# Attention outputs transposed by DMA as 16-bit planes, instead of by TensorE

## Chip, cores and metric

The kernel runs on one core of a Trainium2 chip. The metric is device time in microseconds (us) of one execution; lower is better. TensorE (PE, with PEld for its weight loads), VectorE (DVE), ScalarE (ACT), GpSimd (POOL) and SyncE (SP, which here only issues transfers) each run their own list of instructions in order and wait for each other through semaphores.

## Reference

Two batches of 2048 tokens, width 512, are a gated cross-attention block followed by a quantised feed-forward block:

```python
scores = einsum('bhid,bhjd->bhij', LN(x) @ Wq, ctx @ Wk) * scale      # 16 heads of 32, 77 context rows
x1  = x + tanh(g0) * (softmax(scores) @ (ctx @ Wv)) @ Wo
xq  = fake_quant_int8(LN(x1), one scale from max|LN(x1)| over everything)
h   = fake_quant_int8(silu(xq @ Wgate_q.T) * (xq @ Wup_q.T), one scale from max|h|)
out = x1 + tanh(g1) * (h @ Wdown_q.T)          # weights quantised to int8, one scale a row
```

The maximum over all of |LN(x1)| has to be known before the first quantised product.

## The kernel before

Three stages follow each other in blocks: attention, gate/up, down. The change lies in the attention block. It handles 32 tiles of 128 tokens in a hand-written software pipeline of slots; each engine has its own function `slot(n, t)`, called for n = 0 to 35 by `tile_slots` (L345): slots 0 to 3 and 20 on are written out, slots 4 to 19 are a hardware loop of 4 rounds of 4 slots, in which semaphore values are computed from the loop register.

In slot n TensorE does, in this order: the first half of the scores of tile n; the transpose of the outputs of tile n-2 (`out_transpose`, L1028: four 128x128 transposes from `o_sb` into PSUM `p_x`); two of the three groups of transposes of the probabilities of tile n-1 (`prob_transpose`, L994); half of the queries of tile n+2; the outputs of tile n-1 for the first 8 heads; the second half of the scores of tile n; the last group of transposes; the other half of the queries; the outputs of the other 8 heads; and the projection by Wo of tile n-2 (`project`). Products that need float32 precision are three products of high and low parts (`three`).

VectorE works through the same slot: `scores_max` and `scores_sub` (subtracts the row maximum and writes `prob[t % 2][:, half, :]`; L701) for half 0, the addition of the projection to x1, `bn_stats` of x1, the low part of the transposed outputs (`out_part`, L722 on), the row maximum of a gate/up weight row block `w_in`, the normalised outputs of tile n-1 (`outputs_rec`, `outputs_norm`, L714), then the same for half 1, the maximum of |LN(x1)| (`xmax`), the low part of the queries, the statistics of tile n+6 and the low part of the transposed tokens (`x_part`). In slots 22 to 29 there are instead parts of the quantisation of the down weights (`down_part`), in even slots the maxima (k = 0), in odd slots the int8 values (k = 1).

ScalarE writes high parts, copies the transposed probabilities (`pT`), takes the exponentials, and writes |LN(x1)| of tile n-4 into PSUM `p_y` (`xabs`, L188).

From tile 8 on the normalised tokens are transposed by DMA: GpSimd splits the float32 tile `xn` into two planes of 16 bits in `xpl_u` (`x_split`, L458), SP transposes the planes back into `xn` in 16-bit units (`planes_transposed`, L371), and ScalarE joins the planes again to float32 (`x_join`, L556). SP's queue holds these transposes in one order with the loads of weight rows (`rows`), their transposes (`rows_transposed`), and in slots 21 to 29 the loads (`down_rows`, three transfers) and stores (`down_stored`) of the down weights.

GpSimd also computes the deviations (`deviation`, `deviation2`) and casts the int8 weights to bfloat16 (L506, L515); before the second cast of a down row block it waits for the store of the first, since both use `w_bf`.

Of the kernel before, what the change touches and what calls it, by code (L numbers as in the profile page):

```python
# [5 lines left out]
F32 = mybir.dt.float32  # L6
# [10 lines left out]
P = 128  # L17
B = 2
S = 2048
D = 512  # L20
# [47 lines left out]
PLANES_FREE = NT - 4  # L68
# [3 lines left out]
def flamingo_block(nc, x, ctx_in, mask, g_xattn, g_ffn, Wq, Wk, Wv, Wo, clip_x, clip_down,  # L72
# [8 lines left out]
    with top:  # L81
# [11 lines left out]
        sb, _, sem = tensors(top)  # L93
        x1 = sb("x1", [P, NT, D])
# [16 lines left out]
        with attn:  # L111
# [17 lines left out]
            with work:  # L129
# [5 lines left out]
                prob = [sb(f"prob{i}", [P, 2, HW]) for i in range(2)]  # L135
                pT = sb("pT", [P, 2 * KB, P])
                o_sb = sb("o_sb", [P, D])
# [45 lines left out]
                xpl_planes = xpl_u[:, :].rearrange("p (two n) -> p two n", two=2)  # L183
# [3 lines left out]
                def xabs(m):  # L187


                    return xpl[:, :] if isinstance(m, int) and m >= PLANES_FREE - 4 else p_y[:, :]  # L190

# [37 lines left out]
                t_warm = sem("t_warm")  # L229
# [81 lines left out]
                a_xpl = sem("a_xpl")  # L311
                g_wbf = sem("g_wbf")
# [11 lines left out]
                def wait(eng, sem_, value):  # L324

                    if not isinstance(value, int) or value > 0:
                        eng.wait_ge(sem_, value)  # L327

# [33 lines left out]
                def _(sp):  # L362
# [8 lines left out]
                    def planes_transposed(n):  # L371
                        sp.wait_ge(g_xpl, n - DIRECT + 1)
                        sp.dma_start_transpose(xn_u[:, :].rearrange("p (c n) -> p c n", n=P),
                                               xpl_u[:, :]).then_inc(d_xT, 16)
# [48 lines left out]
                    planes_transposed(NW + 3)  # L423
# [18 lines left out]
                    planes_transposed(NW + 4)  # L442
                    for r in range(KD):
                        if WD0 + 2 * r + 5 < NT:
                            planes_transposed(WD0 + 2 * r + 5)
# [4 lines left out]
                        if WD0 + 2 * r + 6 < NT:  # L450
                            planes_transposed(WD0 + 2 * r + 6)
                        down_stored(r, WC - 1)
                    sp.wait_ge(d_wT, 16 * NW)
# [3 lines left out]
                def _(pool):  # L457
                    def x_split():  # L458
                        pool.tensor_copy(xpl_planes, xn_pairs).then_inc(g_xpl, 1)

                    def deviation(n, t, split=False):
# [4 lines left out]
                        if split:  # L466
                            wait(pool, a_xn, n)
                            wait(pool, v_xlo, n - 1)
                        else:
                            wait(pool, a_xn, n - 1)  # L470
                        pool.tensor_tensor(ve[:, :], mv[:, 1:2], eps[:, :], ALU.add).then_inc(g_self, 1)
                        pool.tensor_tensor(nmean[:, :], mv[:, 0:1], minus[:, :], ALU.mult).then_inc(g_self, 1)
                        if split:
                            x_split()
# [5 lines left out]
                    def deviation2(m):  # L480
# [7 lines left out]
                        wait(pool, g_self2, 3 * m + 3)  # L488
                        pool.tensor_tensor(nb2[:, span(m)], nmean2[:, :], rs2[:, span(m)], ALU.mult)\
                            .then_inc(g_nb2, 1)  # L490

                    def slot(n, t):
                        if runs(n + 5, NT):
                            deviation(n + 5, t + 5, split=joined(n + 4))
                        elif runs(n + 4, NT):
                            wait(pool, a_xn, n + 5)
                            wait(pool, v_xlo, n + 4)
                            x_split()
                        if runs(n - 3, NT):
                            deviation2(n - 3)  # L500
# [40 lines left out]
                def _(act):  # L541
# [13 lines left out]

                    def x_join(n, t):  # L556
                        wait(act, d_xT, (n - DIRECT) * 16 + 16)
                        act.copy(xpl_pairs, xn_planes).then_inc(a_xpl, 1)
# [9 lines left out]
                    def slot(n, t):  # L568
                        if runs(n - 2, NT):
                            wait(act, t_oT, n - 1)  # L570
                            if not last_tile(n - 2):
# [1047 lines left out]
```

## Time and profile before

| | |
|---|---|
| median of 3 runs | 642.82 us (642.26 to 643.49) |
| the profiled execution, its own time | 643.5 us |
| its span | 641.7 us |
| PE busy | 623.3 us (97%) |
| DVE busy | 510.4 us (80%) |
| ACT busy | 352.6 us (55%) |
| POOL busy | 197.2 us (31%) |
| attention block, slots 4 to 19 | 71.36 to 249.03 us |
| attention block, slots 22 to 29 | 271.26 to 360.17 us |

Busy shares are averages over three stages with different limits, and a busy PE is one that has instructions in flight. A row of busy time by stretch has: the stretch, its length, busy us and instructions (x) of PE, PEld, DVE, ACT and POOL, the granted clock of TensorE (1.00 is 2.4 GHz), the mean busy share of the DMA engines, GB/s. In a timeline the second column is the duration of one instruction; neighbours on an engine overlap a little, so the difference of two starts says what an instruction takes of its engine's time.

### The profile page before, as it was taken

Reading aid. Unit: us, or ns where it says so; the run is one execution under the profiler, and the core shown is the slowest. Engines: PE = TensorE matmul, PEld = TensorE weight load, DVE = VectorE, ACT = ScalarE, POOL = GpSimd, SP = SyncE. Lnnn points to the kernel's source line nnn. Section 1 sums busy time; section 2 is a strip of 40 time slices with the busy share of each in tenths; the row PEclk is TensorE's granted clock in tenths of the full one; section 3 lists DMA queues with packets and bytes.
Section 4 is the critical chain, followed back from the end, with each engine's and each line's share of the span. In section 5 each row is a group of like instructions: output and inputs, shape, how many; then the busy total and the mean of one; then the engine's idle time right before and its main releaser. Section 6 shows DMA issues by size and latency. Waiting matters only on the chain. (4 is left out here: it accounts for less than half of the span.)

```text
span 641.7 us, 12724 instructions
## 1 busy us (share of the span) xinstructions
PE 623.3 (97%) x3912; PEld 471.1 (73%) x3912; DVE 510.4 (80%) x954; ACT 352.6 (55%) x512; POOL 197.2 (31%) x416
## 2 busy tenths in 40 slices
PE   8969999999999999999999997999999999899997
PEld 6769999999999999999999995444444444444544
DVE  6586889888888989899887766788888888866764
ACT  5254465667666565666664343555555554365653
POOL 7021333333333333232320211201111110056775
PEclk9999999999999999999999998999999999999999
DMA  8739222222222223313411000276446110099723
GB/s 311 193 80 335 59 52 59 65 57 65 58 65 50 63 51 59 90 39 85 95 33 60 25 0 1 49 226 211 135 145 212 25 32 9 1 344 394 275 105 126
DMA packets 85206, 69.61 MB, mean 108 GB/s; under 512 B 64915, under 2 KB 67373, under 8 KB 85165
## 3 DMA queue, kind: packets, MB, share of 16 engines
q1 hardware_dynamic: 80259, 52.33, 29.1%
q10 hardware_dynamic: 4906, 16.78, 7.4%
q8 instruction: 21, 0.34, 0.2%
q14 instruction: 20, 0.16, 0.1%
HBM read 32.48 MB, written 21.36 MB: 84 GB/s over the span
## 5 line engine op out<-in xcount | busy, mean ns | idle before, releaser
L1298 ACT ACTIVATE sb_silu<-ps_g,sb_sgu 128x512 f32<-128x512 f32 x88 | 60.5, 687 | 72.1 <-PE ps_g L1385 43.8
L1385 PE MATMUL ps_g<-sb_xqT,sb_wgu 128*128 128x512 bf16 x352 | 90.3, 379 | 0.6 <-DVE sb_xqT L1341 0.6
L1385 PE MATMUL ps_u<-sb_xqT,sb_wgu 128*128 128x512 bf16 x352 | 90.3, 379 | 0.0
L589 ACT COPY sb_pT<-ps_p 128x512 f32<-128x512 f32 (+1 forms) x96 | 46.5, 520 | 71.3 <-PE ps_p L1002 71.3
L1356 DVE SCALAR_TENSOR_TENSOR sb_h<-ps_u,sb_sgu,sb_silu 128x512 f32<-128x512 f32 (+1 forms) x88 | 66.0, 751 | 19.4 <-PE ps_u L1385 18.3
L1013 PE MATMUL ps_o<-sb_vblk,sb_pT 128*128 (+4 forms) x640 | 79.0, 270 | 1.2 <-ACT sb_pT L589 1.2
L1013 PEld LDWEIGHTS ps_o<-sb_vblk,sb_pT 128*128 128x128 f32 (+1 forms) x640 | 76.8, 191 | 1.8 <-ACT sb_pT L589 1.4
L946 PE MATMUL ps_q<-sb_xT_hi,sb_wq_hi 128*128 128x256 f32 x256 | 77.5, 303 | 0.0
L698 DVE TENSOR_REDUCE sb_smax<-ps_s 128x8 f32<-128x616 f32 x64 | 51.1, 799 | 26.8 <-PE ps_s L991 26.4
L948 PE MATMUL ps_q<-sb_xT_hi,sb_wq_lo 128*128 128x256 f32 x256 | 72.3, 282 | 0.0
L947 PE MATMUL ps_q<-sb_xT_lo,sb_wq_hi 128*128 128x256 f32 x256 | 72.2, 282 | 0.0
L1591 PE MATMUL ps_z<-sb_wdT,sb_hq 128*128 128x512 bf16 x330 | 71.7, 380 | 0.0
L1466 POOL TENSOR_TENSOR sb_wgu<-sb_wgu,sb_x 128x512 f32<-128x512 f32 x31 | 53.7, 1734 | 53.5 <-DVE sb_wgu L1523 53.0
L1360 DVE TENSOR_REDUCE sb_hmax<-sb_h 128x1 f32<-128x512 f32 (+1 forms) x88 | 60.4, 686 | 8.0 <-DVE sb_h L1356 0.7
L1385 PEld LDWEIGHTS ps_g<-sb_xqT,sb_wgu 128*128 128x128 bf16 x352 | 34.4, 98 | 42.1 <-ACT sb_xqT L1312 0.8
L1385 PEld LDWEIGHTS ps_u<-sb_xqT,sb_wgu 128*128 128x128 bf16 x352 | 34.4, 98 | 41.5
L1591 PEld LDWEIGHTS ps_z<-sb_wdT,sb_hq 128*128 128x128 bf16 x330 | 32.4, 98 | 39.1 <-issue 0.8
L1486 ACT CAST sb_hq<-sb_h 128x1408 bf16<-128x1408 int8 (+1 forms) x32 | 42.0, 1311 | 28.9 <-DVE sb_h L1516 28.3
L593 ACT ACTIVATE sb_prob<-sb_prob 128x616 f32<-128x616 f32 x64 | 46.2, 721 | 16.1 <-DVE sb_prob L704 16.1
L704 DVE TENSOR_TENSOR sb_prob<-ps_s,sb_smax 128x616 f32<-128x616 f32 x64 | 50.8, 793 | 2.7
L1281 POOL CAST sb_xqb<-sb_xq 128x512 bf16<-128x512 int8 x28 | 17.2, 613 | 111.8 <-ACT sb_xq L1290 95.4
L946 PE MATMUL ps_y<-sb_wo_hi,sb_oT_hi 128*128 128x512 f32 x124 | 51.4, 414 | 0.0
(218 smaller groups left out, 1349.8 us busy)
## 6 DMA issues: line engine op xcount, KB each, us to landing
h_spill<-sb_h SPq DMA_DIRECT2D x4, 2816.0 KB, 8.8
sb_h<-h_spill ACTq DMA_DIRECT2D x16, 704.0 KB, 6.7
out_dram<-sb_wgu SPq DMA_DIRECT2D x31, 256.0 KB, 2.2
sb_x<-in_x_dram ACTq DMA_DIRECT2D x1, 4096.0 KB, 17.0
sb_w_in<-in_L_ffn_w_gate_dram SPq DMA_DIRECT2D x11, 256.0 KB, 2.6
sb_w_in<-in_L_ffn_w_up_dram SPq DMA_DIRECT2D x11, 256.0 KB, 2.6
sb_x<-in_x_dram SPq DMA_DIRECT2D x2, 1024.0 KB, 14.1
sb_x<-in_x_dram SPq DMA_DIRECT2D x2, 512.0 KB, 4.7
```

The lines of the kernel that those rows point to most:

```text
L698: dve.tensor_reduce(smax[:, half, :].rearrange("p (g h) -> p g h", g=2), half_scores(), X, ALU.max).then_inc(v_max, 1)
L704: dve.tensor_tensor(prob[t % 2][:, half, :].rearrange("p (g h m) -> p g h m", g=2, h=HG), half_scores(), smax[:, half, :].rearrange("p (g ...
L946: pe.matmul(o, hi, rhi, start=first, stop=False)
L947: pe.matmul(o, hi, rlo, start=False, stop=False)
L948: return pe.matmul(o, lo, rhi, start=False, stop=last)
L1013: last = pe.matmul(p_o[:, first:end + 1, :].rearrange("p h d -> p (h d)"), pT[rows, half * KB + j, :], vblk[rows, span(b), half, SLOT0[j]: ...
L1298: act.activation(silu[(j * KI + i) % 2][:, :, :].rearrange("p t n -> p (t n)"), p_g[(j * KI + i) % 2][:, :], ACT.Silu, scale=sgu[:, i:i + ...
L1356: dve.scalar_tensor_tensor(steps_h, p_u[(j * KI + i) % 2][:, :, :], sgu[:, KI + i:KI + i + 1], silu[(j * KI + i) % 2][:, :, :], ALU.mult, ...
L1360: dve.tensor_reduce(hmax[:, span(u)], steps_h, mybir.AxisListType.XY, ALU.max, apply_absolute_value=True).then_inc(v_hmax, 1)
L1385: last = pe.matmul(banks[(j * KI + i) % 2][:, :], wgu[:, what, k, i * P:(i + 1) * P], xqT[j][:, k, :], start=(k == 0), stop=(k == KD - 1))
L1466: pool.tensor_tensor(yd[k], yd[k], x1[:, span((v + RT) % NT), :].rearrange("p a d -> p (a d)"), ALU.add).then_inc(g_out, 1)
L1591: last = pe.matmul(p_z[k % 4][:, :], hq[k % 4][:, i, :], wdT[:, i, :], start=(i == 0), stop=(i == KI - 1))
```

## The change

Tiles 2 to 29 (`O_FIRST`, `O_END`) are no longer transposed by TensorE. Their outputs lie in `o_sb`, seen as 16-bit words. GpSimd splits each half (8 heads) into planes (`out_split`), which lie in half 0 of the probabilities' buffer of the same parity; SP transposes each half by a DMA of its own (`out_transposed`) back into `o_sb`; ScalarE joins both halves into `xpl` (`out_join`) and makes the high part from it. The token tile's planes now lie in half 1 of the probabilities' buffer, and |LN(x1)| too, instead of PSUM `p_y` or `xpl`. Some work is put in another order: on ScalarE the first exponential and |LN(x1)|, on VectorE the weight row's maximum, `out_part`, `xmax`. Unused semaphores go.

```diff
@@ SP
+                    def out_transposed(m, half):
+                        sp.wait_ge(g_opl, 2 * (m - O_FIRST) + half + 1)
+                        sp.dma_start_transpose(o_pairs(half).rearrange("p (c n) -> p c n", n=P),
+                                               o_planes(m, half)).then_inc(d_oT, 16)
+
+                    def slot_transposes(n):
+                        if o_joined(n - 2):
+                            out_transposed(n - 2, 1)
+                        if DIRECT <= n + 4 < NT:
+                            planes_transposed(n + 4)
+                        if o_joined(n - 1):
+                            out_transposed(n - 1, 0)
@@ order on SP: weights up to slot 22, then the down weights
                         rows_transposed(w - 2)
-                        if w + 3 >= DIRECT:
-                            planes_transposed(w + 3)
+                        slot_transposes(w - 1)
                         rows(w)
...
                     down_rows(0)
-                    planes_transposed(NW + 4)
+                    slot_transposes(NW)
                     for r in range(KD):
-                        if WD0 + 2 * r + 5 < NT:
-                            planes_transposed(WD0 + 2 * r + 5)
+                        slot_transposes(WD0 + 2 * r + 1)
                         for q in range(WC - 1):
                             down_stored(r, q)
                         if r + 1 < KD:
                             down_rows(r + 1)
-                        if WD0 + 2 * r + 6 < NT:
-                            planes_transposed(WD0 + 2 * r + 6)
+                        slot_transposes(WD0 + 2 * r + 2)
                         down_stored(r, WC - 1)
@@ GpSimd
+                    def out_split(t, half):
+                        pool.tensor_copy(o_planes(t, half).rearrange("p (two n) -> p two n", two=2),
+                                         o_pairs(half).rearrange("p (n two) -> p two n", two=2)).then_inc(g_opl, 1)
...
+                        wait(pool, a_xn, n - 1)
+                        if o_ready:
+                            wait(pool, v_o, 2 * (n - 6))
+                        pool.tensor_tensor(ve[:, :], mv[:, 1:2], eps[:, :], ALU.add).then_inc(g_self, 1)
+                        if o_ready:
+                            out_split(t - 7, 1)
+                        if x_ready:
                             wait(pool, a_xn, n)
+                            wait(pool, t_p, 3 * (n - 6))
+                            wait(pool, v_xmax, n - 8)
...
                         pool.tensor_tensor(nb2[:, span(m)], nmean2[:, :], rs2[:, span(m)], ALU.mult)\
                             .then_inc(g_nb2, 1)
+                        if o_joined(m + 2):
+                            out_split(t + 2, 0)
@@ ScalarE
+                    def out_join(m):
+                        wait(act, d_oT, 32 * (m - O_FIRST + 1))
+                        wait(act, v_xlo, min(m + 6, NT) if isinstance(m, int) else m + 6)
+                        act.copy(xpl_halves, o_halves).then_inc(a_opl, 1)
+                        wait(act, a_opl, m - O_FIRST + 1)
+                        wait(act, t_y, m)
+                        act.copy(oT(m)[0], xpl_T).then_inc(a_ohi, 1)
@@ VectorE, scores_sub
+                        if half == 0 and o_joined(n - 2):
+                            wait(dve, d_oT, 32 * (n - 1 - O_FIRST))
+                        if half == 1:
+                            wait(dve, v_xmax, n - 3)
+                        if half == 1 and runs(n + 4, NT) and joined(n + 4):
+                            wait(dve, d_xT, 16 * (n + 5 - DIRECT))
@@ VectorE, outputs_norm
-                        wait(dve, t_oT, n)
+                        if o_joined(n - 1):
+                            wait(dve, a_opl, n - O_FIRST)
@@ VectorE, slot: the weight row's maximum now stands ahead of scores_sub(n, t, 0), out_part behind
@@ outputs_norm(n - 1, 0), the reduction for xmax behind scores_sub(n, t, 1)
@@ TensorE
-                        if not isinstance(m, int) or m < PLANES_FREE - 2:
-                            wait(pe, v_xmax, m)
...
-                        if runs(n - 2, NT - 1):
+                        if runs(n - 2, NT - 1) and not o_joined(n - 2):
                             out_transpose(n - 2)
```

## Rows read from the trace of the kernel before

**Rows 1.** Busy time by engine in slots 4 to 19 and 22 to 29.

```profile
71.36:249.03 177.67, 177.67 (x1313) 169.27 (x1312) 152.69 (x320) 113.87 (x176) 63.98 (x174) 1.00 0.26 60
...
271.26:360.17 88.91, 88.91 (x658) 84.64 (x657) 78.14 (x163) 51.72 (x82) 25.56 (x69) 1.00 0.25 65
```

**Rows 2.** Timeline of PE, slot 19: start us, duration us, instruction.

```profile
238.77 0.60 PE L1036 MATMUL ps_x<-sb_identf,sb_o_sb 128*128 128x128 f32 x4
239.21 1.04 PE L1002 MATMUL ps_p<-sb_identf,sb_prob 128*128 128x128 f32 x8
...
242.54 0.39 PE L989 MATMUL ps_s<-sb_k_hi,sb_q_hi 128*128 x1
```

**Rows 3.** Timeline of DVE, slot 19.

```profile
240.50 0.80 DVE L704 TENSOR_TENSOR sb_prob<-ps_s,sb_smax 128x616 f32<-128x616 f32 x1
...
242.40 0.67 DVE L818 TENSOR_REDUCE sb_w_am<-sb_w_in 128x1 f32<-128x512 f32 x1
243.00 0.17 DVE L822 BATCH_NORM_AGGREGATE sb_mvt<-sb_bn 128x2 f32<-128x6 f32 x1
...
247.49 0.42 DVE L717 TENSOR_TENSOR sb_o_sb<-ps_o,sb_rden 128x256 f32<-128x256 f32 x1
247.83 0.17 DVE L663 BATCH_NORM_AGGREGATE sb_mv<-sb_bn 128x2 f32<-128x6 f32 x1
248.87 0.69 DVE L676 TENSOR_TENSOR sb_xT_lo<-sb_xpl,sb_xT_hi 128x512 fp32r<-128x512 f32 x1 [0.87 <-ACT sb_xT_hi L561]
```

**Rows 4.** Timeline of POOL behind that instruction.

```profile
249.79 0.19 POOL L471 TENSOR_TENSOR sb_ve<-sb_mv,sb_eps 128x1 f32<-128x1 f32 x1 [3.87 <-DVE sb_xT_lo L676]
```

**Rows 5.** POOL's 16-bit split and a cast of 512 columns, by shape.

```profile
L459 POOL COPY sb_xpl<-sb_xn 128x1024 uint16<-128x1024 uint16 x24 | 24.9, 1036 | 5.1 <-DVE sb_xT_lo L676 5.1
...
L515 POOL CAST sb_w_bf<-sb_vblk 128x512 bf16<-128x512 int8 x4 | 2.5, 614 | 7.8 <-DMA wd_spill<-sb_w_bf 7.8
```

**Rows 6.** DMA transposes of the page: count, median us from issue to landing.

```profile
sb_xn<-sb_xpl SPq DMA_TRANSPOSE x24, 3.1
...
sb_wgu<-sb_w_bf SPq DMA_TRANSPOSE x22, 2.6
```

**Rows 7.** ACT's join of the token planes.

```profile
L558 ACT COPY sb_xpl<-sb_xn 128x1024 uint16<-128x1024 uint16 x24 | 32.3, 1346 | 0.0
```

**Rows 8.** Timeline of DVE, slots 23, 24 and 26: first subtraction, second normalisation.

```profile
284.85 0.80 DVE L704 TENSOR_TENSOR sb_prob<-ps_s,sb_smax 128x616 f32<-128x616 f32 x1
...
288.14 0.80 DVE L698 TENSOR_REDUCE sb_smax<-ps_s 128x8 f32<-128x616 f32 x1 [0.25 <-PE ps_s L991]
...
292.40 0.42 DVE L717 TENSOR_TENSOR sb_o_sb<-ps_o,sb_rden 128x256 f32<-128x256 f32 x1
...
295.96 0.80 DVE L704 TENSOR_TENSOR sb_prob<-ps_s,sb_smax 128x616 f32<-128x616 f32 x1
...
304.15 0.42 DVE L717 TENSOR_TENSOR sb_o_sb<-ps_o,sb_rden 128x256 f32<-128x256 f32 x1
...
318.19 0.80 DVE L704 TENSOR_TENSOR sb_prob<-ps_s,sb_smax 128x616 f32<-128x616 f32 x1
...
325.81 0.42 DVE L717 TENSOR_TENSOR sb_o_sb<-ps_o,sb_rden 128x256 f32<-128x256 f32 x1
```

**Rows 9.** Timeline of SP's queue, end of slot 23 and start of slot 24.

```profile
292.06 0.43 SPq L431 DMA_DIRECT2D sb_w_in<-in_L_ffn_w_down_dram  x1
...
293.02 0.43 SPq L431 DMA_DIRECT2D sb_w_in<-in_L_ffn_w_down_dram  x1
295.70 1.23 SPq L373 DMA_TRANSPOSE sb_xn<-sb_xpl  x1
```

**Rows 10.** Stretch in which these loads move (columns as in Rows 1).

```profile
292.40:295.80 3.40, 3.40 (x26) 3.17 (x25) 2.47 (x5) 2.54 (x5) 1.43 (x4) 1.00 0.79 248
```

**Rows 11.** DVE's int8 instructions of 512 columns, by shape, 80 to 340 us.

```profile
L742 DVE TENSOR_SCALAR sb_vblk<-sb_vblk,sb_wd_inv 128x512 int8<-128x512 f32 x3 | 1.8, 607 | 0.0
...
L742 DVE TENSOR_SCALAR sb_w_i<-sb_w_in,sb_wd_inv 128x512 int8<-128x512 f32 x3 | 1.4, 477 | 0.0
```

More of the change, by code:

```diff
@@ L134, in flamingo_block @@
                 xn = xn_u[:, :].bitcast(F32)
-                prob = [sb(f"prob{i}", [P, 2, HW]) for i in range(2)]
+                prob_u = [sb(f"prob{i}", [P, 2, 2 * HW], U16) for i in range(2)]
+                prob = [a[:, :, :].bitcast(F32) for a in prob_u]
                 pT = sb("pT", [P, 2 * KB, P])
-                o_sb = sb("o_sb", [P, D])
+                o_u = sb("o_sb", [P, 2 * D], U16)
+                o_sb = o_u[:, :].bitcast(F32)
                 oT_hi = sb("oT_hi", [P, KD, P], F32R)
@@ L576, in slot @@
                         for c, (k0, k1) in enumerate(CHUNKS):
-                            if c == 2 and runs(n - 4, NT - 1):
-                                wait(act, g_nb2, n - 3)
-                                wait(act, v_xmax, n - 3)
-                                if isinstance(n, int) and n >= PLANES_FREE:
-                                    act.wait_ge(v_xlo, NT)
-                                else:
-                                    wait(act, v_x1, n - 2)
-                                act.activation(xabs(n - 4), row(n - 4), ACT.Abs, bias=nb2[:, span(n - 4)],
-                                               scale=rs2[:, span(n - 4)]).then_inc(a_abs, 1)
+                            if c == 2 and runs(n - 2, NT) and o_joined(n - 2):
+                                out_join(n - 2)
+                            if c == 2 and runs(n, NT):
+                                exponential(n, t, 0)
                             if runs(n - 1, NT):
@@ L589, in slot @@
                                 act.copy(pT[:, k0:k1, :], p_p[c % 2][:, 0:k1 - k0, :]).then_inc(a_p, 1)
-                        for half in range(2):
-                            if runs(n, NT):
-                                wait(act, v_sub, 2 * n + half + 1)
-                                act.activation(prob[t % 2][:, half, :], prob[t % 2][:, half, :], ACT.Exp,
-                                               scale=SCALE).then_inc(a_exp, 1)
-                            if half == 0 and runs(n + 2, NT):
-                                q_part(n + 2, (t + 2) % 4)
+                        if runs(n - 4, NT - 1):
+                            wait(act, g_nb2, n - 3)
+                            wait(act, v_xmax, n - 3)
+                            wait(act, t_p, 3 * min(n, NT) if isinstance(n, int) else 3 * n)
+                            act.activation(xabs(t), row(n - 4), ACT.Abs, bias=nb2[:, span(n - 4)],
+                                           scale=rs2[:, span(n - 4)]).then_inc(a_abs, 1)
+                        if runs(n + 2, NT):
+                            q_part(n + 2, (t + 2) % 4)
+                        if runs(n, NT):
+                            exponential(n, t, 1)
                         if runs(n + 4, NT):
@@ L830, in slot @@
                             outputs_norm(n - 1, 0)
+                        if runs(n - 2, NT - 1) and o_joined(n - 2):
+                            out_part(n - 2)
                         if runs(n, NT):
@@ L1063, in slot @@
                             scores(n, t, 0)
-                        if runs(n - 2, NT - 1):
+                        if runs(n - 2, NT - 1) and not o_joined(n - 2):
                             out_transpose(n - 2)
```

113 lines of the change are left out of this document (69 added, 44 removed).

## The prediction

> **What bounds the kernel now.** I first read the busy time of each engine by stretch, cut at the starts of slots. In slots 4 to 19 TensorE is busy for all 177.67 us, in slots 22 to 29 for all 88.91 us [rows 1], with a granted clock of 1.00 (2.4 GHz): a slot is 177.67 / 16 = 11.10 us there and 88.91 / 8 = 11.11 us here. So TensorE sets the pace of the attention block, and only what leaves its list shortens it. VectorE is close behind: 152.69 / 16 = 9.5 us a slot in the first stretch, 78.14 / 8 = 9.8 us in the second. Next the timelines of single slots, for the distances between VectorE's instructions, because the new waits tie these into a circle; last the transfers, with their time from issue to landing.
>
> **What goes.** The four transposes of the outputs start 0.44 us before the next group (238.77, 239.21) [rows 2]. TensorE has no gap around them, so a slot of TensorE would take 11.10 - 0.44 = 10.66 us. It happens in slots 4 to 31, 28 times: 12.3 us at most.
>
> **What comes, and the circle.** `scores_sub(n, t, 0)` now waits until both halves of tile n-2 have been transposed, since their planes lie in the buffer that it writes. The second half of tile n-2 is normalised at the end of slot n-1. Call S the start of the first subtraction and N the start of the second normalisation in a slot. Then S, VectorE's list up to N, split, transpose, and the next S follow each other, and the period of a slot is the longer of TensorE's 10.66 us and this circle.
>
> S to N is 247.49 - 240.50 = 6.99 us in slot 19 [rows 3]. The weight row's maximum is moved ahead of S: 243.00 - 242.40 = 0.60 us less, so 6.39 us.
>
> N to the next S, written-out slots: normalisation and aggregate 247.83 + 0.17 - 247.49 = 0.51 [rows 3]; the hand-over to POOL 249.79 - (248.87 + 0.69) = 0.23 [rows 3, 4], say 0.2; POOL's first small instruction 0.15 (0.19 long [rows 4]); the half's split between half of the whole one, 0.52, and a cast of 512 columns, 0.61: 0.6, as an instruction has a fixed part [rows 5]; the transpose 2.6, as the weights' have the same 128x512 elements (the token's, twice as large, take 3.1 [rows 6]; 2.6 is the nearest); SP's start and VectorE's release about 0.1 (estimate). Together 4.2 us, bounds 3.6 (less at both hand-overs and 0.2 us less in flight) and 4.8 (a transpose as slow as the large one). In the loop three more waits with computed values stand behind the one that ends last; I add 0.15, between 0 and 0.35 (estimate).
>
> The half's split on POOL also meets VectorE's int8 instruction. Where such an instruction met a cast on POOL it took 607 ns, otherwise 477 [rows 11]; I add 0.13, between 0 and 0.4.
>
> Slots 4 to 19: 6.39 + 0.13 + 4.35 = 10.87 us, just above TensorE's 10.66. Gain 11.10 - 10.87 = 0.23, x 16 = 3.7 us (bounds 0 and 7.0). Slot 20 gains 0.4, slots 30 and 31, where VectorE has much less to do, 0.44 each: together 5.0 us.
>
> **Slots 21 to 29.** Here VectorE has the down weights' work between S and N. Even slots: 304.15 - 295.96 = 8.19 in slot 24 [rows 8], + 4.2 = 12.39, which is 1.28 us over 11.11; slots 22 and 24: +2.6. Slots 26 and 28 have no token statistics: 325.81 - 318.19 = 7.62 [rows 8], and the split waits for no aggregate: 3.95; 11.57, +0.46 each: +0.9.
>
> Odd slots: 292.40 - 284.85 = 7.55, less the 0.25 us in which VectorE waited for scores [rows 8]. But SP's queue comes later than this. The three loads of the next down rows start 292.06 - 284.85 = 7.21 us behind S [rows 8, 9]. In front of the first store now stand a split (0.6) and the issue of a transpose (1.23 [rows 9], 0.6 of it beyond the cast), while `out_part` is gone from VectorE's list there (-0.5): the loads start at S + 7.9 and occupy SP's queue to S + 9.35 (293.02 + 0.43 - 292.06 = 1.4 [rows 9]). Only then can the second half be issued. Landing, if its data meet nothing: 9.4 + 2.6 + 0.1 = S + 12.1. If they stand behind the loads, whose data moved from 292.4 to 295.8 [rows 10], so to S + 11.65: + (2.6 - 1.23) + 0.1 = 13.1. I take 13.0, as all sit in one queue: +1.9 us for slots 23, 25 and 27, +5.7. Slot 29 has no loads behind it: -0.3. Slot 21 has the loads for row block 0 in the same place: +1.0 (bounds -0.4 and +1.5). Together 2.6 + 0.9 + 5.7 - 0.3 + 1.0 = 9.9 us.
>
> The Trainium skill ("DMA: Bandwidth & Descriptors", Two DMAs through the same engine are not ordered) says that descriptors of one queue of a DMA engine start in order. By that the half stands behind the loads, 13.1; no row here has a transpose right behind loads.
>
> **What costs nothing, and its cover.** ACT gets a second join of 1.35 us [rows 7]: 51.72 / 8 + 1.35 = 7.8 us of a slot of over 10.6 [rows 1]. `out_join` ends about 2.1 us behind the landing; VectorE comes to `out_part` 2.0 us behind S, and TensorE's projection is more than 2 us later. POOL's two splits, 1.2 us, are added to 64 / 16 = 4 us. On TensorE the subtraction has 242.54 - 241.30 = 1.24 us before the second scores [rows 2, 3]; 0.44 and 0.60 of that go, and 0.2 is left: a late landing reaches TensorE almost at once. The token's planes are issued behind the half, 1.2 us later than the earliest; their reader on VectorE comes some 4 us after S. |LN(x1)| from SBUF instead of PSUM, the renamed semaphores and the moved exponential: 0.
>
> **Sum.** 9.9 - 5.0 = +4.9 us on the profiled execution, 643.5 to 648.4. The median of the runs is 0.7 us below it, so 647.5 us. What a measurement here can tell from no change is about 0.2%, 1.3 us.
>
> **Rivals.**
> 1. Faster: the half's way is short. At N to S of 3.6 us slots 4 to 19 are bound by TensorE (16 x 0.44 = 7.0, with slots 20, 30 and 31 8.3); slots 22 and 24 cost 1.4, 26 and 28 -0.3, the odd ones 3.9 (the loads' data less in the way), 21 and 29 nothing: 5.0. Net -3.3: 639.5 us. It decides below about 3.95 us. For it: two of the terms are bounds from other shapes. Against it: 2.6 us of it is measured 22 times [rows 6].
> 2. The new waits don't reach TensorE anywhere: 28 x 0.44, 630.5 us. Against it: 8.19 us from S to N leaves 2.5 us for a 2.6 us transpose.
> 3. The circle is longer, since VectorE and POOL get into each other's way. VectorE's `x_part` (0.69 us, both inputs in SBUF) starts 248.87 - 247.49 = 1.4 us behind N [rows 3], after the change about 0.8, because the second exponential comes earlier; the split would start at N + 1.0. If the split waits for it to end, 0.45 us are added in 16 slots and 0.33 in slots 22, 24 and 26: +8.2, 655.7 us. Neither for nor against it is there a row with such a pair; the 607 ns above speak for some cost. The Trainium skill ("SBUF — State Buffer", Who interferes with whom) has it as a rule that a VectorE instruction with two SBUF inputs contends with a GpSimd instruction that reads SBUF, and that the second one blocks; by it this rival is what happens.
> 4. Both halves nearly cancel: slots 4 to 19 reach TensorE's pace, the down slots cost what I say: -8.3 + 9.9, or a little less; 641.5 to 644.1.
>
> **Chances.** Forecast (644.1 to 651) 0.45; longer circle (above 651) 0.18; short way (637 to 641.5) 0.20; near cancelling 0.12; nothing reaches TensorE 0.05. Faster 0.25, same 0.12, slower 0.63. The range must take in most of the longer circle, to 656, and most of the short way, from 639; what is left out is the last case and the outer ends. The forecast's own range is 644 to 651.
>
> **What would show it.** TensorE idle in front of the second scores (L989), released by the subtraction; VectorE idle in front of the first subtraction, released by the transpose into `o_sb`; slot lengths of 10.7 to 11.0 us in slots 4 to 19, some 12.4 and 13.0 in turn in slots 22 to 25; PE busy in the second stretch well under its length. The half's split at 0.6 us, its landing at 2.6. The prediction is wrong if N to S is below 4 us, or if the down slots take 11 us.

## The result, and the profile after the change

The changed kernel takes 658.9 us (median of 4 runs, 657.6 to 661.9) against 642.7 us (642.3 to 643.5) for the kernel before: a ratio of 1.0258, 95% interval 1.0231 to 1.0286. It is slower by 16.2 us, where 4.8 us were forecast and the range ended at 656. The profiled execution is the longest of the four, 661.85 us with a span of 659.7 us; before, the span was 641.7 us.

S is the start of the first subtraction of a slot and N that of the second normalisation, as in the prediction. From S of slot 4 to S of slot 31 the trace before shows 372.68 - 73.94 = 298.74 us, the one after 389.33 - 72.44 = 316.89 us: 18.15 us more, as much as the spans differ by (18.0 us). Ahead of slot 4 the trace after is 1.5 us shorter and behind S of slot 31 1.35 us longer (269.02 and 270.37 us), which nearly cancels, so the loss lies between slots 4 and 31. Busy time by engine of the changed kernel, slots 4 to 19, 20 and 21, 22 to 30 (columns as in [rows 1]):

```profile
72.44:251.58 179.14, 175.02 (x1251) 164.71 (x1250) 153.81 (x321) 136.51 (x193) 94.25 (x208) 0.99 0.40 82
251.58:275.34 23.76, 22.78 (x169) 21.57 (x168) 19.89 (x40) 17.17 (x25) 11.02 (x26) 1.00 0.46 103
275.34:380.03 104.69, 93.80 (x620) 88.87 (x620) 78.52 (x163) 62.25 (x90) 38.34 (x80) 0.90 0.30 69
```

In [rows 1] TensorE was busy for the whole of both stretches. Now it is idle for 4.1 us of the first stretch, 1.0 us of the second and 10.9 us of the last, and its granted clock in the last is 0.90. The waits of the changed kernel (total us, times, longest us) name the instruction:

```profile
DVE sb_prob L775 <- DMA sb_o_sb<-sb_prob: 27.5, 22, 4.2
PE ps_s L1066 <- DVE sb_prob L775: 18.1, 12, 3.4
```

VectorE's subtraction waits for the transpose into `o_sb`, and TensorE's second scores for the subtraction. Slot 10 shows the circle at rest. Timelines of DVE, of POOL and of SP's queue:

```profile
142.14 0.80 DVE L775 TENSOR_TENSOR sb_prob<-ps_s,sb_smax 128x616 f32<-128x616 f32 x1 [0.44 <-DMA sb_o_sb<-sb_prob]
...
148.57 0.42 DVE L791 TENSOR_TENSOR sb_o_sb<-ps_o,sb_rden 128x256 f32<-128x256 f32 x1
148.91 0.17 DVE L728 BATCH_NORM_AGGREGATE sb_mv<-sb_bn 128x2 f32<-128x6 f32 x1
149.36 0.69 DVE L741 TENSOR_TENSOR sb_xT_lo<-sb_xpl,sb_xT_hi 128x512 fp32r<-128x512 f32 x1 [0.28 <-ACT sb_xT_hi L630]
...
153.05 0.80 DVE L775 TENSOR_TENSOR sb_prob<-ps_s,sb_smax 128x616 f32<-128x616 f32 x1 [0.44 <-DMA sb_o_sb<-sb_prob]
```

```profile
149.25 0.19 POOL L504 TENSOR_TENSOR sb_ve<-sb_mv,sb_eps 128x1 f32<-128x1 f32 x1 [2.00 <-DVE sb_mv L728]
149.38 1.15 POOL L493 COPY sb_prob<-sb_o_sb 128x512 uint16<-128x512 uint16 x1
```

```profile
150.55 1.19 SPq L397 DMA_TRANSPOSE sb_o_sb<-sb_prob  x1
```

S to N is 6.43 us (predicted 6.39). N to S is 4.48 us: 0.68 to POOL's start, 0.13 for its small instruction, 1.15 for the split, 2.5 from issue to landing. The split takes nearly twice the 0.6 us of the sum, and it starts while VectorE's `x_part` with two inputs in SBUF runs. The period is 10.91 us. Slots 9, 13, 14, 17 and 18 look the same. In slots 8, 11, 12, 15 and 16 POOL's small instruction is the one beside `x_part`: it takes 0.67 us in slot 8 and 0.69 us in slot 11, and the split 0.60 and 0.61. In slot 19 POOL begins first, and VectorE's instruction is the long one:

```profile
248.34 0.61 POOL L493 COPY sb_prob<-sb_o_sb 128x512 uint16<-128x512 uint16 x1
...
248.40 1.10 DVE L741 TENSOR_TENSOR sb_xT_lo<-sb_xpl,sb_xT_hi 128x512 fp32r<-128x512 f32 x1 [0.28 <-ACT sb_xT_hi L630]
```

Slot 23 is one of the three that cost most. SP's queue, POOL and DVE:

```profile
292.09 1.19 SPq L397 DMA_TRANSPOSE sb_o_sb<-sb_prob  x1
293.33 3.05 SPq L468 DMA_DIRECT2D wd_spill<-sb_w_bf  x2
296.42 0.43 SPq L462 DMA_DIRECT2D sb_w_in<-in_L_ffn_w_down_dram  x1
...
297.39 0.43 SPq L462 DMA_DIRECT2D sb_w_in<-in_L_ffn_w_down_dram  x1
297.87 1.19 SPq L397 DMA_TRANSPOSE sb_o_sb<-sb_prob  x1
```

```profile
291.46 0.61 POOL L493 COPY sb_prob<-sb_o_sb 128x512 uint16<-128x512 uint16 x1
292.01 0.81 POOL L564 CAST sb_w_bf<-sb_w_i 128x512 bf16<-128x512 int8 x1
295.40 0.61 POOL L564 CAST sb_w_bf<-sb_vblk 128x512 bf16<-128x512 int8 x1 [2.58 <-DMA wd_spill<-sb_w_bf]
...
296.55 0.61 POOL L493 COPY sb_prob<-sb_o_sb 128x512 uint16<-128x512 uint16 x1
```

```profile
287.75 0.80 DVE L775 TENSOR_TENSOR sb_prob<-ps_s,sb_smax 128x616 f32<-128x616 f32 x1 [1.00 <-DMA sb_o_sb<-sb_prob]
...
301.92 0.80 DVE L775 TENSOR_TENSOR sb_prob<-ps_s,sb_smax 128x616 f32<-128x616 f32 x1 [4.06 <-DMA sb_o_sb<-sb_prob]
```

In front of the second half stand the issue of the first half, the first store, POOL's second cast (which waits 2.58 us for that store to land), the second store and the three loads. The half is issued 297.87 - 287.75 = 10.12 us behind S, and the next S starts 4.05 us after the issue.

### The profile page after: what moved, and what is told of

It is laid out like the page before. It is cut to its first block and busy times, and to the rows that moved or that the text cites. A ratio compares the mean times of both kernels' runs of the same rounds, so it can differ in the third digit from the quotient of the medians.

```text
span 659.7 us, 12770 instructions
## 1 busy us (share of the span) xinstructions
PE 622.3 (94%) x3779; PEld 467.5 (71%) x3800; DVE 512.6 (78%) x954; ACT 391.6 (59%) x540; POOL 247.8 (38%) x472
## 5 line engine op out<-in xcount | busy, mean ns | idle before, releaser
L1023 PE MATMUL ps_q<-sb_xT_hi,sb_wq_hi 128*128 128x256 f32 x256 | 80.2, 313 | 0.0
L1025 PE MATMUL ps_q<-sb_xT_hi,sb_wq_lo 128*128 128x256 f32 x256 | 74.6, 291 | 0.0
L1024 PE MATMUL ps_q<-sb_xT_lo,sb_wq_hi 128*128 128x256 f32 x256 | 74.6, 291 | 0.0
L1066 PE MATMUL ps_s<-sb_k_hi,sb_q_hi 128*128 128x308 f32 (+1 forms) x128 | 43.5, 339 | 20.4 <-DVE sb_prob L775 18.1
L619 ACT COPY sb_xpl<-sb_o_sb 128x1024 uint16<-128x1024 uint16 x28 | 37.7, 1348 | 34.0 <-DMA sb_o_sb<-sb_prob 34.0
```

The lines of the kernel that those rows point to most:

```text
L1023: pe.matmul(o, hi, rhi, start=first, stop=False)
L1024: pe.matmul(o, hi, rlo, start=False, stop=False)
L1025: return pe.matmul(o, lo, rhi, start=False, stop=last)
```

## The experiments

All times are medians; each ratio is against the kernel before on the same chip (642.2 to 642.5 us). The changed kernel's 658.9 us were measured beside 642.7 us for the kernel before, so up to 0.5 us of a difference between a version and the changed kernel can come from that. The expectations name the experiments by labels: 1 is e1_end19, 2 e2_rest_alone, 3 e3_split_first, 4 e5_xpart_waits, 5 e4_half_before_loads, 9 e9_split_end19, 10 e10_best and 12 e12_both_queues. Slot lengths are those from S to S in each run's own trace.

**1. Fewer joined tiles.**

```diff
-O_FIRST, O_END = 2, NT - 2
+O_FIRST, O_END = 2, 19
```

> The changed kernel with its list of joined tiles cut to 2 to 18 (O_END = 19 instead of 30); tiles 19 to 31 are transposed by TensorE again, everything else stays. Theory (the loss arises in the slots with down weights, through the wait of the first subtraction on the outputs' halves): slots 4 to 19 take 10.9 to 11.2 us as in the changed kernel (11.10 before), slots 20 to 30 take 11.1 us again: about 2 us under the kernel before, 640.5 us; 644 if the long slots 5 to 7 (11.9 to 12.6 us) of the profiled run return. Rival (the loss comes from the other parts, the token's planes and |LN(x1)| in the probabilities' buffer, or the moved exponential): slots 21 to 29 stay long, 655 us or more.

Measured 642.4 us (ratio 0.9998, 0.9978 to 1.0018). Slots 21 to 29 are back at 11.1 us (slot 21 at 10.63). Slots 4 to 19 take 179.00 us, as in the changed kernel, with the long slots 5 to 7 (11.71, 12.55, 11.92). So the down slots carry 16.5 us, the whole difference between this kernel and the changed one, and the loop's slots, predicted to gain 3.7 us, lose 1.4. The theory of the slots held. The other parts were tested by themselves:

**2. Everything but the outputs.** `o_joined` is false for every tile.

> No outputs are joined at all (all tiles' outputs are transposed by TensorE); what is left of the change is the token's planes and |LN(x1)| in the probabilities' buffer, the weight row's maximum ahead of the first subtraction and the exponential in front of the third chunk. Theory: these cost nothing, 642.7 us within 1.3. Rival: they carry a part of the 16 us; then this kernel shows that part.

Measured 641.95 us, ratio 0.9999 (0.9989 to 1.0008): the token's planes and |LN(x1)| in the probabilities' buffer and the moved exponential, weight row's maximum and `xmax` cost nothing. `out_part` has its new place only for joined tiles, so this run doesn't test that.

**3. The split ahead of the statistics.**

```diff
+    if o_ready:
+        wait(pool, v_o, 2 * (n - 6))
+        pool.tensor_tensor(dum[:, :], eps[:, :], minus[:, :], ALU.mult)
+        out_split(t - 7, 1)
     wait(pool, v_st, n + 1)
...
-    if o_ready:
-        out_split(t - 7, 1)
```

> In slots 4 to 26 POOL splits the second half as soon as it is normalised, ahead of its wait for the token's statistics and of the first small instruction (one small instruction carries the wait). Theory (the circle sets the slots, and the split is long because it runs beside VectorE's x_part with both inputs in SBUF: 1.15 us instead of 0.60): split 0.60 us, second normalisation to first subtraction 3.8 us instead of 4.45; slots 4 to 19 fall from 10.9 to TensorE's 10.66, slots 21, 22 and 24 by 0.7 each, the odd down slots hardly: about 6 us less than the changed kernel, 652.5 us. First rival (the meeting only moves to another instruction of VectorE): 0.35 us less in the circle, 655 us. Second rival (TensorE or the clock sets slots 4 to 19): within 1 us of 658.9.

Measured 655.2 us, ratio 1.0208 (1.0188 to 1.0229). Slots 8 to 19 fall from 131.57 to 128.43 us, 10.70 each, and slots 4 to 7 from 47.57 to 44.98. Slots 21 and 22 stay at 12.89 and 12.39, where 0.7 less was expected, slot 24 grows from 12.40 to 13.31 (its clock is 0.74, see experiment 7), and the odd down slots stay at 13.6 to 15.5. The total lies at the first rival's, but the trace tells the two apart: in slots 9 to 11, 13 to 15 and 17 to 19 the split takes 0.61 us and it is VectorE's `x_part` that is stretched, to 0.99 to 1.01 us, without making S late. The meeting has moved, as the rival says, but out of the circle, as the theory says; only in slots 4, 8, 12 and 16 is the split still 1.13 to 1.14 us. What is missing from the total is missing in the down slots.

**4. `x_part` behind the split.** The order on POOL is unchanged; only the meeting is taken away.

```diff
     if runs(n + 4, NT):
+        if o_joined(n - 1):
+            wait(dve, g_opl, 2 * (n - O_FIRST))
         x_part(n + 4, t)
```

> The changed kernel, but VectorE's x_part in slots 4 to 27 starts only when POOL has split the second half of the outputs, so the two never run at once; POOL's order is that of the changed kernel. Theory (the split takes 1.15 instead of 0.60 us because of an instruction of VectorE with both inputs in SBUF beside it, and the circle sets the slots): split 0.60 us, second normalisation to first subtraction about 4.0 us instead of 4.45, slots 4 to 19 10.66 instead of 10.9, slots 22 and 24 0.45 less: 5 us less than the changed kernel, 654 us. Rival (the split is long for another reason, or x_part is so late that the queries wait for it): the split stays above 1 us or the time within 1 us of 658.9.

Measured 651.2 us, ratio 1.0127 (1.0107 to 1.0148), 7.7 us under the changed kernel, where 5 were expected. DVE and POOL in slot 11 of this kernel:

```profile
156.11 0.42 DVE L791 TENSOR_TENSOR sb_o_sb<-ps_o,sb_rden 128x256 f32<-128x256 f32 x1
...
157.72 0.69 DVE L741 TENSOR_TENSOR sb_xT_lo<-sb_xpl,sb_xT_hi 128x512 fp32r<-128x512 f32 x1 [1.10 <-POOL sb_prob L493]
...
160.23 0.79 DVE L775 TENSOR_TENSOR sb_prob<-ps_s,sb_smax 128x616 f32<-128x616 f32 x1
```

```profile
157.07 0.61 POOL L493 COPY sb_prob<-sb_o_sb 128x512 uint16<-128x512 uint16 x1
157.84 0.62 POOL L511 TENSOR_TENSOR sb_nmean<-sb_mv,sb_minus 128x1 f32<-128x1 f32 x1 [0.15 <-issue]
```

The split is back at 0.61 us although `x_part` is as long as before (0.69); the stretching has moved to a small instruction that nobody waits for (0.62 instead of 0.19), and S waits no more. N to S is 4.12 us. Slots 8 to 19 take 127.84 us, 10.65 each, TensorE's pace; slots 4 to 7 fall from 47.57 to 43.91 us. Of the long slots only slot 6, 11.62 us, is left. The edit takes the meeting away from the split and, to do so, starts `x_part` some 0.7 us later. In slots 8 to 19 the gain of 3.73 us fits the meeting. About as much, 3.66 us, lies in slots 4 to 7, and these are not steady: with the same wait they take 44.21 us in experiment 12 and 46.29 us in experiment 13. So that part of the 7.7 us isn't shown to be the meeting's alone. Slots 22 and 24 were to fall by 0.45 us each; slot 22 falls to 12.18, slot 24 grows to 13.65 us. In it TensorE is busy at a clock of 0.75 (window with TensorE alone):

```profile
295.37:309.02 13.65, 12.70 (x71) 0.75 0.23 41
```

**5. The second half in front of the loads.**

```diff
+    if o_joined(WD0 + 2 * r):
+        out_transposed(WD0 + 2 * r, 1)
     if r + 1 < KD:
         down_rows(r + 1)
-    slot_transposes(WD0 + 2 * r + 2)
+    slot_transposes(WD0 + 2 * r + 2, first=False)
```

and the same around `down_rows(0)`.

> In the queue that issues all of these transfers the second half of the outputs is issued in front of the three loads of the next down rows (in slots 20, 21, 23, 25, 27 and 29), not behind them. Theory (the odd down slots are long because the half waits behind the loads and is issued 10.1 us after the first subtraction): slots 23, 25 and 27 fall from 14.2 to 14.9 us to about 12.4, slot 21 by 0.4; TensorE's idle times of 3.3 us shrink to about 1.7 and the granted clock stays at 1.00, so slots 26 and 28 fall from 12.3 to 11.6: 8 us less, 651 us. Rival (the loads come too late for the next row block's first maximum): as much is given back in the even slots, 657 to 659 us.

Measured 659.0 us, ratio 1.0277 (1.0248 to 1.0307). Slots 21, 23, 25 and 27 fall to 10.81, 12.02, 12.01 and 11.46 us, and the even ones rise to 14.45, 14.23, 13.72 and 14.12: the rival. DVE in slot 22:

```profile
273.60 0.80 DVE L778 TENSOR_TENSOR sb_prob<-ps_s,sb_smax 128x616 f32<-128x616 f32 x1 [0.82 <-DMA sb_o_sb<-sb_prob]
277.08 0.69 DVE L811 TENSOR_REDUCE sb_wd_am<-sb_w_in 128x1 f32<-128x512 f32 x1 [2.08 <-DMA sb_w_in<-in_L_ffn_w_down_dram]
```

The loads are now the late ones. Their first reader stands between S and N, so its wait of 2.08 us is in the circle in the next slot.

**6. No loads.**

```diff
 def down_rows(r):
     if r:
-        sp.wait_ge(v_wd8, WC * r)
+        return
...
-    if q == 0:
+    if q == 0 and r == 0:
         dve.wait_ge(l_wd[r], 16 * WC)
```

> The changed kernel without the loads of the down rows of row blocks 1 to 3 (the maxima and the int8 instructions run on row block 0's rows again, so the down weights of the other blocks are left out), and without the wait for them. Theory (the odd slots are long because the three loads stand in front of the second half in the issuing queue, in half_before_loads the same time came back as a wait for the loads): slots 23, 25 and 27 take about 12.4 us (the half is issued 8.3 to 8.7 us behind the first subtraction instead of 10.1), the even slots 12.4 as before, slots 26 and 28 11.6 without the clock's fall: 7 us less than the changed kernel, 652 us. Rival (the stores in front of the loads hold the queue as long): 14 us stay, 657 us or more.

Measured 652.7 us, ratio 1.0155 (1.0134 to 1.0177), 6.2 us under the changed kernel. Slots 23, 25 and 27 take 12.01, 11.59 and 13.02 us, slots 24, 26 and 28 12.56, 11.77 and 11.26. From S of slot 22 to S of slot 31 this trace is 8.4 us shorter (105.59 instead of 113.99). With the loads SP's wait for VectorE's int8 instructions in front of them is gone too, so the 8.4 us are those of both. Slot 27 stays at 13.02 us without any load: its second half is issued 9.3 us behind S and the next S starts 3.70 us later, so the loads aren't all that makes it long.

**7. TensorE kept busy.**

```diff
+    if isinstance(n, int) and n in (24, 26, 28):
+        for _ in range(12):
+            last = pe.matmul(p_x[:, :, :].rearrange("p k n -> p (k n)"), identb[:, :],
+                             identb[:, :].unsqueeze(1).broadcast_to([P, 4, P]), start=True, stop=True)
+        last.then_inc(t_warm, 1)
     if runs(n, NT):
         scores(n, t, 1)
```

> The changed kernel with 12 matmuls of 128x512 (bf16, the identity) into an unused PSUM bank in front of the second scores of slots 24, 26 and 28, where TensorE otherwise stands idle for 3.3 us behind the odd down slots. Theory (these idle times let the granted clock fall to 0.5 for some us, and the slower TensorE then keeps slots 26 and 28 at 12.3 us instead of 11.6): clock 1.00 in slots 23 to 29, slots 26 and 28 about 11.6, the odd slots unchanged at 14.2 to 14.9: 1.5 to 2.5 us less, 656.9 us. Rival (the clock costs nothing, as the circle sets these slots too): 658.9 within 0.7.

In the changed kernel TensorE stands idle at the start of slots 24 and 26, and its clock is 0.86 in slot 24, 0.75 in slot 26 and 0.74 in slot 28 (timeline, then windows of slots 26 and 28 with TensorE alone):

```profile
302.87 0.38 PE L1066 MATMUL ps_s<-sb_k_hi,sb_q_hi 128*128 128x308 f32 x1 [3.30 <-DVE sb_prob L775]
329.50 0.60 PE L1066 MATMUL ps_s<-sb_k_hi,sb_q_hi 128*128 128x308 f32 x1 [3.36 <-DVE sb_prob L775]
```

```profile
328.55:340.79 12.24, 11.29 (x63) 0.75 0.19 36
...
355.68:368.01 12.33, 11.38 (x63) 0.74 0.13 29
```

With the matmuls, the same two slots:

```profile
331.47:343.24 11.77, 10.97 (x79) 1.00 0.16 35
...
358.10:369.35 11.25, 10.31 (x75) 1.00 0.14 32
```

Slots 26, 28 and 29 take 11.77, 11.25 and 11.41 us instead of 12.24, 12.33 and 12.02: 2.2 us. Slot 24, whose clock rises from 0.86 to 1.00 as well, stays at 12.38 us (12.40): there the circle is as long. In slot 29 the clock is 1.00 in both kernels; its 0.6 us are TensorE no longer being behind (it was busy for all of the 12.02 us, and for 10.97 of the 11.41). The median is 657.6 us (ratio 1.0227, 1.0205 to 1.0249), which by itself isn't distinguishable from the changed kernel's; the trace shows the term, the time only agrees with it.

**8. A buffer of its own for the second half's planes,** tiles 2 to 18 joined: `o_planes` of the second half lies in `w_in2`, `scores_sub` waits for the first half only, and the two halves count on separate semaphores.

> Joined tiles 2 to 18 only, as in e1_end19, and the planes of the second half of tiles 2 to 17 lie in a buffer of their own (unused until slot 20), so that the first subtraction waits for the first half's transpose alone. Theory (that subtraction's wait on the second half is what sets slots 4 to 19): VectorE no longer waits there, slots 4 to 20 take TensorE's 10.66 us, also the long slots 5 to 7 (11.7 to 12.6 in e1_end19) come near it: 8 us less than e1_end19, 635 us. Rival (the circle closes as well through ScalarE's join, for which the next tile's first normalisation waits): landing 4.4 us behind the second normalisation, a join of 1.35, and 1.7 us to 6.4 us from first subtraction by way of the first normalisation to the second: 10.5 us, no longer than 10.66, but slots 5 to 7 stay long: 638 to 640 us.

Measured 639.7 us, ratio 0.9954 (0.9937 to 0.9972), within the rival's range and by its mechanism. Slots 8 to 18 take 10.85 us on average, so the circle by way of the join is longer than the rival's 10.5 and still sets them; slots 5 and 7 stay long (12.26 and 11.63). DVE and ACT in slot 9:

```profile
132.32 0.42 DVE L800 TENSOR_TENSOR sb_o_sb<-ps_o,sb_rden 128x256 f32<-128x256 f32 x1 [0.49 <-ACT sb_xpl L626]
```

```profile
130.86 1.36 ACT L626 COPY sb_xpl<-sb_o_sb 128x1024 uint16<-128x1024 uint16 x1 [1.29 <-DMA sb_o_sb<-sb_w_in]
```

Freed of the planes' buffer, the circle closes through the join: the next tile's first normalisation may not write `o_sb` before ScalarE has read it.

**9 and 10. Versions for speed:** tiles 2 to 18 with the split first, and tiles 2 to 18 with `x_part` behind the split.

> Joined tiles 2 to 18 only (e1_end19) with the second half split first on POOL (e3_split_first). Theory: slots 8 to 20 take 10.7 us, slots 5 and 6 still 11.7, slots 21 to 31 as before the change: 177.6 - 173.4 = 4.2 us from slots 4 to 19 and 0.4 from slot 20: 638 us, faster than the kernel before by 0.7 per cent. Rival (the gain that the slots show is given back behind the attention block, as in e2_rest_alone and e1_end19, whose times hardly differ though their slots 4 to 20 differ): 641 to 642.5 us.

> Joined tiles 2 to 18 (e1_end19) and x_part behind the split (e5_xpart_waits). Slots 4 to 19 as in e5_xpart_waits, 171.8 us against 177.6 before, slot 20 0.4 less, slots 21 to 31 as before: 6.2 us under the kernel before, 636 us, and 1.5 to 2 us under e9_split_end19 (637.7). Rival (the split's place no longer matters once the down slots are left out): 637.7.

Measured 637.7 us (0.9920, 0.9904 to 0.9936) and 636.9 us (0.9916, 0.9899 to 0.9933). Both are faster than the kernel before and the changed one; between the two the time can't tell. Windows of the second kernel, slots 4 to 19 and 20 to 30:

```profile
73.80:245.64 171.84, 170.84 (x1250) 162.27 (x1250) 150.96 (x321) 137.31 (x193) 93.49 (x208) 1.00 0.42 85
245.64:365.89 120.25, 120.25 (x887) 114.33 (x886) 103.24 (x215) 71.36 (x112) 34.95 (x91) 1.00 0.23 59
```

171.84 / 16 = 10.74 us a slot: TensorE sets the pace again, on a shorter list.

**11. The loop begins at slot 8,** slots 4 to 7 written out, otherwise as the last.

> e10_best with slots 4 to 7 written out too, the loop running over slots 8 to 19. Theory A (slots 5 to 7 are long, 11.0 and 11.6 us with x_part behind the split and 11.9 and 12.6 in the changed kernel, because the loop's instructions are fetched in its first pass, which holds up the transposes): the long slots move to 9 and 10, and the sum stays within 0.7 us of e10_best. Theory B (something else of that stretch of time makes them long): they stay at slots 5 and 6.

Measured 638.6 us (0.9943, 0.9923 to 0.9964), 1.8 us above the last kernel where at most 0.7 was expected. The long slots are now 7 and 8 (11.88 and 12.70), where the last kernel had slot 6 (12.03); slots 4 to 6 take 10.94, 10.83 and 10.77. So they moved when the loop's start did, but by one or two slots for its four, and not to 9 and 10: neither theory as it stands. Transfers of the changed kernel between 84 and 96 us and of this one between 120 and 132 us (count, KB, us to landing; the queue called instruction: packets, MB, share):

```profile
q8 instruction: 1, 0.02, 1.1%
sb_w_in<-in_L_ffn_w_gate_dram SPq DMA_DIRECT2D x1, 256.0 KB, 5.1
...
sb_wgu<-sb_w_bf SPq DMA_TRANSPOSE x1, 5.0
```

```profile
q14 instruction: 3, 0.02, 1.6%
q8 instruction: 1, 0.02, 0.5%
sb_w_in<-in_L_ffn_w_gate_dram SPq DMA_DIRECT2D x1, 256.0 KB, 5.0
sb_o_sb<-sb_prob SPq DMA_TRANSPOSE x2, 3.5
sb_wgu<-sb_w_bf SPq DMA_TRANSPOSE x1, 5.5
```

In quiet slots these transfers land in 3.0, 2.5 and 2.8 us. Fetches of instructions lie in the long slots of both kernels, but not only there: between 72 and 84 us the changed kernel has one packet on each of the two queues, and the same transfers land in 2.9, 2.5 and 2.8 us. What goes with the longest slot is the three packets on q14 (96 to 108 us in the changed kernel and in the kernel of experiment 10, 120 to 132 us here). That fetches cause the delay is argued from their place, not shown.

**12 and 13. All tiles joined, the queue reordered.** Both have `x_part` behind the split, the second half in front of the loads, and VectorE's three maxima of a down row block behind the second subtraction. The second also issues the token's planes in front of the loads.

> Joined tiles 2 to 29 with everything that the runs so far point to: x_part behind the split (e5_xpart_waits), the second half issued in front of the down rows' loads (e4_half_before_loads), and VectorE's three maxima of a down row block behind the second subtraction, so that the later landing of the loads is not waited for. Theory: odd slots 12.0 as in e4_half_before_loads, even slots 11.6 to 12.2 instead of 14.2, no fall of the clock: slots 21 to 29 cost 0.9 us each over 11.11 and slots 4 to 20 gain 6 us: 643 to 645 us, so the down slots can be brought near the others but still give back what the loop's slots gain. Rival (a further wait takes the place of the two): above 648 us.

> e12_both_queues with the token's planes issued in front of the loads too, so the order is second half, planes, loads, first half. In e12_both_queues VectorE waited 1.5 us before the second subtraction of slots 22 and 24 for the planes' landing. Theory (what is left is the queue's order): that wait goes, slots 22 and 24 fall from 13.65 and 13.96 to about 12.3, 26 from 12.75 to 11.6, the odd ones stay at 11.5: 4 us less than e12_both_queues, 642 to 643 us, a floor that VectorE's 8.1 us from first subtraction to second normalisation and the 4.1 us of split and transpose set. Rival (the loads now land so late that the maxima wait): the even slots keep above 13 us, 645 us or more.

The first: 646.3 us (1.0066, 1.0051 to 1.0082), between the theory's range and the rival's. Slots 23, 25 and 27 take 11.59, 11.57 and 11.46 us, slots 22, 24 and 26 still 13.65, 13.96 and 12.75, with a third wait in place of the other two, DVE in slot 22:

```profile
272.17 0.80 DVE L778 TENSOR_TENSOR sb_prob<-ps_s,sb_smax 128x616 f32<-128x616 f32 x1 [1.51 <-DMA sb_xn<-sb_prob]
```

The second: 643.9 us (1.0020, 1.0001 to 1.0038), with single runs from 640.7 to 648.1; the trace is of the longest, and in it slots 6 and 7 alone take 2.5 us more than in the first (24.98 against 22.44). Slots 22 and 24 are 13.09 and 13.19 us, where 12.3 was expected; in slot 22 the maxima now wait 0.80 us for the loads. Slot 26 is 11.63 and slot 27 13.04. Theory and rival each hold for a part, and slots 22 and 24 did not come down to 12.3 us.

## Why the prediction was wrong

The direction and the wait that sets the pace were right, the size was not: 16.2 us instead of 4.8, and slots 4 to 19 lost where they were to gain. By the prediction's terms, in the two traces (the one after is of the longest run, so the sum is 2 us above the difference of the medians; slot 31 lies behind the stretch measured):

| slots | predicted | measured |
|---|---|---|
| 4 to 19 | -3.7 | 179.14 - 177.57 = +1.6 |
| 20, 30 and 31 | -1.3 | -0.19 - 0.74 = -0.9 (20 and 30 alone) |
| 21 | +1.0 | 12.83 - 11.11 = +1.7 |
| 22, 24 | +2.6 | 24.81 - 22.23 = +2.6 |
| 23, 25, 27 | +5.7 | 43.29 - 33.33 = +10.0 |
| 26, 28 | +0.9 | 24.57 - 22.24 = +2.3 |
| 29 | -0.3 | 12.02 - 11.10 = +0.9 |
| sum | +4.9 | +18.2 |

- **The odd down slots (4.3 us of the miss).** The step that failed is "the loads start at S + 7.9 and occupy SP's queue to S + 9.35". They started at S + 8.67 and ended at S + 10.07, and the second half was issued at S + 10.1 to 10.2 instead of 9.4. The sum took 0.5 us off because `out_part` leaves VectorE's list in front of POOL's work. VectorE's aggregate did come earlier, at S + 1.96 instead of 2.30, but `out_part` in its new place reads both inputs from SBUF and runs beside POOL's third small instruction, which took 0.93 us instead of 0.55. So POOL came to the first half's split at S + 3.71, no earlier than to its cast before (3.72). POOL of the kernel before, then DVE and POOL of the changed one:

```profile
287.82 0.55 POOL L487 TENSOR_TENSOR sb_rs<-sb_ve,sb_mhalf 128x1 f32<-128x1 f32 x1
...
290.17 0.68 DVE L801 TENSOR_TENSOR sb_oT_lo<-sb_xpl,sb_oT_hi 128x512 fp32r<-128x512 f32 x1
290.33 0.93 POOL L526 TENSOR_TENSOR sb_rs<-sb_ve,sb_mhalf 128x1 f32<-128x1 f32 x1
```

With the split and the issue in front of it the first store came 1.2 us later (S + 5.58 instead of 4.36; the sum had 0.7), and POOL's second cast, which waits for that store to land, began 2.07 us behind the store's issue instead of 1.82. The second store, the three loads and the second half follow in the queue. That is 2.2 of the 4.3 us. The other 2.1 us are the way from the half's issue to the next S: 4.05, 4.14 and 4.68 us in slots 23, 25 and 27 where the sum had 3.6; in slot 23 of experiment 5, without loads ahead of it, it took 2.59 us (297.48 to 300.07). The Trainium skill ("DMA: Bandwidth & Descriptors", Two DMAs through the same engine are not ordered) says that descriptors in one queue of one DMA engine start in order; the 4.05 against 2.59 us agree with it.

- **Slots 4 to 19 (5.3 us).** A quiet slot was predicted at 10.87 us and measured at 10.91. That it came so near is luck, since two errors cancel inside it: the split's meeting with VectorE cost 0.55 us instead of 0.13, and from issue to S it took 2.50 us where the sum had 2.6, 0.1 for SP and VectorE and 0.15 for the loop's computed waits. Those last two terms were estimates that no run measures by themselves. The misses are slots 5 to 7, 36.35 us against 32.61 (+3.7), and the first slot of each round of the loop, 11.23 us against 10.87 (4 x 0.36 = 1.4); in that slot S to N is the longer part, 6.81 us in slot 8 against 6.43. In the kernel before, TensorE hid both: every slot had 11.1 us whatever a transfer or the loop's turn did. A circle that is as long as TensorE's list has no such reserve.
- **Rival 3, which had 0.18, is real in its mechanism.** Experiments 3 and 4 take the meeting away from the split in two ways, and in both slots 8 to 19 fall to TensorE's pace (10.70 and 10.65 us). The prediction left out most of it because no row had such a pair. The Trainium skill ("SBUF — State Buffer", Who interferes with whom) has the rule that the second of the two blocks: here POOL's split started at 149.38, behind VectorE's 149.36, and it was the one that took 1.15 us; in slot 19 VectorE started behind POOL (248.40 and 248.34) and took 1.10 us, so the traces agree. But the meeting alone doesn't explain the loss: without it 9 us were left.
- **The clock (2.2 us, in the trace).** The prediction has no such term. TensorE's idle time behind an odd slot is followed by a clock of 0.75 and 0.74 in slots 26 and 28, so TensorE sets these at 12.3 us, where the circle had allowed 11.6. How deep the clock falls doesn't follow the idle time: 3.30 us were followed by 0.86 in slot 24 here, and 3.20 and 2.68 us by 0.74 and 0.75 in slot 24 of experiments 3 and 4.
- **Slot 29 (1.2 us).** It was to gain 0.3 us, having no loads. But its second split stands behind POOL's second cast, which waits 3.04 us for a store, and starts 1.70 us behind N where that of slot 28 starts 0.49 us behind it.
- **What was right:** 12.39 us for slots 22 and 24 (12.41 and 12.40), S to N, the place of the waits, and that the other parts cost nothing (experiment 2). The TensorE slot of 10.66 us was met in experiments 3 and 4.

What stays open: why slots 5 to 7 are long, beyond their moving when the loop's start moves; why a half takes 3.7 us from issue to S in slot 27 even without loads; why the clock falls to 0.75 in some even slots and to 0.86 in others; and what fills the last microsecond of slots 22 and 24 in experiment 13.

## What to carry to other kernels

A wait that closes a circle through several engines takes the reserve out of every step in it: sum the circle for each kind of slot, the first of a loop round and the first pass included, and ask what is hidden today only because another engine is slower. For a transfer that goes into a shared issuing queue, walk the queue's whole order with each entry's own wait; moving one entry forward makes the next one late, three times in a row here. Where a change costs in some stages and gains in others, apply it only where it gains: with the tiles cut to 2 to 18 and one wait that keeps VectorE's two-input instruction off POOL's copy it gives 636.9 us, 0.8 per cent less than before.

## What was not expected of the hardware

- A copy of 512 16-bit columns on POOL took 0.61 us alone and 1.15 us when it began 0.02 us behind a VectorE instruction of 0.69 us with both inputs in SBUF; a one-column instruction in the same place took 0.62 instead of 0.19 us (experiment 4). VectorE's took 0.69 us in these cases. Where the copy began 0.06 us ahead (slot 19), it took 0.61 us and VectorE's instruction 1.10.
- After TensorE had been idle for 3.30 and 3.36 us the granted clock of the following slot was 0.86 and 0.75 (1.00 is 2.4 GHz, 0.50 is 1.2 GHz, and the figure is the slot's mean); with matmuls in the gaps it was 1.00.
- A transpose and a load that land in 2.8 and 3.0 us in quiet slots took 5.0 and 5.1 us in the changed kernel's slot 5, in the loop's first pass, and 5.5 and 5.0 us in slot 8 with the loop starting there (experiment 11). Single transfers late elsewhere exist too: one such transpose took 4.4 us between 84 and 96 us in experiment 11. The cause is open.
